# Adaptive-norm transformer layer on one Trainium2 core: the feed-forward part a slot later, local values from whole probabilities and a value difference, gate logits in column strips, and a split rank product

## The reference, cut to what matters

```python
h = layernorm(x) * (1 + ca) + sa
x = x + ga * attention(h)
h = layernorm(x) * (1 + cb) + sb
x = x + gb * feed(h)

# attention(h): q = rope(h @ Wq), k = rope(h @ Wk), v = h @ Wv
#   out_comp: softmax over up to 64 compressed keys (one per 16 tokens), masked, times compressed values
#   out_sel:  softmax over 16 selected tokens (the two blocks of highest mean score), times their values
#   out_win:  softmax over the last 128 tokens (cols <= rows, cols > rows - 128), times v
#   g = softmax(h @ Wg + bg, axis=-1)                      # 3 gates per token
#   out = g[0] * out_comp + g[1] * out_sel + g[2] * out_win
#   return out @ Wo + bo
# feed(h): base = h @ base_W.T + base_b                    # 512 x 512
#   z = h @ [shared_A, routed_A].T                         # 16 + 6 * 16 = 112 columns
#   routed z weighted by the normalised top 2 of 6 router probabilities
#   return base + [z_shared, z_routed * w] @ [shared_B, routed_B].T
```

## Time and profile before

| | |
|---|---|
| median of 3 runs | 2219.99 us (2219.48 to 2226.52) |
| the profiled execution's own time | 2229.21 us |
| its span, first to last instruction | 2227.3 us |
| mean granted TensorE clock | 0.967 of full speed |
| busy share of the span | PE 91%, PEld 66%, DVE 81%, ACT 60%, POOL 39% |

### The profile page before, as it was taken

How to read it: one execution, slowest core, us unless ns; L and a number is a source line. 1 busy time by engine, 2 the same in 40 slices (tenths; PEclk the granted TensorE clock), 3 DMA queues, 4 the chain that set the end, 5 groups by cost and what they waited for, 6 DMA issues and landing times.

```text
span 2227.3 us, 49222 instructions
## 1 busy us (share of the span) xinstructions
PE 2023.9 (91%) x18028; PEld 1465.2 (66%) x18028; DVE 1793.5 (81%) x4806; ACT 1327.9 (60%) x4658; POOL 878.8 (39%) x843
## 2 busy tenths in 40 slices
PE   6988999899999999989999999999999999987876
PEld 3656667666676766667666666766766676665554
DVE  4668888878987888878897788878898788886775
ACT  2346666556665666655666566655666566655654
POOL 1534444334442444334443344434444344432232
PEclk9999999999999999989999999999999999997888
DMA  6210100101011010110001001010001100010000
GB/s 215 63 44 20 30 25 29 44 25 30 20 34 44 20 30 25 33 40 25 25 25 53 15 30 30 30 39 25 29 20 34 44 25 25 29 32 23 20 20 20
DMA packets 43537, 77.56 MB, mean 35 GB/s; under 512 B 7314, under 2 KB 7314, under 8 KB 43299
## 3 DMA queue, kind: packets, MB, share of 16 engines
q1 hardware_dynamic: 32034, 56.85, 8.9%
q10 hardware_dynamic: 11264, 17.57, 2.1%
HBM read 53.38 MB, written 16.83 MB: 32 GB/s over the span
## 4 chain that ended last, share of the span: by engine, by line
PE 51%; DVE 34%; ACT 6%; issue 5%; POOL 2%; DMA 1%; SPq 1%; DVEq 0%; ACTq 0%; POOLq 0%
DVE ps_s L1791 6%; PE ps_o L685 5%; PE ps_t L660 5%; DVE wmax L1796 4%; PE ps_o L715 4%; PE ps_m L558 3%; PE ps_m L560 3%; PE ps_m L559 3%; PE ps_s L679 3%; PE ps_m L755 3%; PE ps_m L773 3%; PE ps_m L774 3%; PE ps_m L782 3%; PE ps_s L636 3%; PE ps_m L790 2%
## 5 line engine op out<-in xcount | busy, mean ns | idle before, releaser
L1182 ACT ACTIVATE pw<-ps_s,wmax 128x128 f32<-128x128 f32 x1024 | 359.3, 380 | 229.6 <-DVE wmax L1796 227.8
L558 PE MATMUL ps_m<-w_hi,h_hi 128*128 128x512 f32 x768 | 340.8, 444 | 8.6 <-DVE h_lo L1927 4.8
L1192 ACT ACTIVATE pw<-pw,wden 128x128 f32<-128x128 f32 x1024 | 313.7, 400 | 30.5 <-DVE wden L1806 30.5
L560 PE MATMUL ps_m<-w_hi,h_lo 128*128 128x512 f32 x768 | 303.2, 395 | 0.0
L559 PE MATMUL ps_m<-w_lo,h_hi 128*128 128x512 f32 x768 | 302.4, 394 | 0.0
L1182 ACT ACTIVATION_READ_ACCUMULATOR pw<-ps_s,wmax 128x1 f32 x1024 | 225.5, 220 | 0.0
L1817 DVE COPY_PREDICATED pT<-keep_prev,ps_t 128x512 f32<-128x512 uint32 x224 | 166.0, 741 | 68.9 <-PE ps_t L660 68.4
L1478 POOL TENSOR_TENSOR css<-css,cden 128x256 f32<-128x256 f32 (+7 forms) x128 | 123.1, 982 | 207.0 <-DVE cden L1856 207.0
L558 PEld LDWEIGHTS ps_m<-w_hi,h_hi 128*128 128x128 f32 x768 | 145.3, 189 | 71.7 <-issue 44.3
L1819 DVE COPY_PREDICATED pT<-keep_own,ps_t 128x512 f32<-128x512 uint32 x256 | 185.3, 724 | 1.0 <-issue 0.3
L685 PE MATMUL ps_o<-pT,v_s 128*32 128x128 f32 x3840 | 168.3, 283 | 13.8 <-DVE pT L1817 8.9
(11 more groups left out here) (213 smaller groups left out, 4791.4 us busy)
## 6 DMA issues: line engine op xcount, KB each, us to landing
xa<-x_in SPq DMA_DIRECT2D x65, 256.0 KB, 2.7
xc<-x_in SPq DMA_DIRECT2D x64, 256.0 KB, 2.7
out<-xc ACTq DMA_DIRECT2D x64, 256.0 KB, 2.0
gbc<-gate_rows SPq DMA_DIRECT2D x24, 256.0 KB, 3.4
pw<-wmod_in SPq DMA_DIRECT2D x3, 1024.0 KB, 8.2
pT<-wmod_in SPq DMA_DIRECT2D x3, 1024.0 KB, 7.2
qT<-wqkv_in SPq DMA_DIRECT2D x2, 1024.0 KB, 13.6
cv_two<-csv SPq DMA_DIRECT2D x16, 128.0 KB, 3.1
```

Source lines behind the costliest of these rows:

```text
L558: pe_.matmul(ps[:], h_hi[:, c, :], w_hi[:, col, c, :], start=(c == 0), stop=False)
L560: mm = pe_.matmul(ps[:], h_lo[:, c, :], w_hi[:, col, c, :], start=False, stop=(c == NC - 1))
L1182: ins = act.activation(pw[:, hw, :], ps_w[:, j, i, 1, :], ACT.Exp, bias=wmax[:, hw:hw + 1], accum_out=wden[:, 0, hw:hw + 1])
L1192: act.activation(pw[:, hw, :], pw[:, hw, :], ACT.Copy, scale=wden[:, 2, hw:hw + 1]).then_inc(wn_ok, 1)
```

## The change

1. **Feed-forward part a slot later.** `transpose_z`, `feed`, `feed_low`, `feed_up`, `final` and `store` of a tile move from the slot of its `output` to the next one and stand at its head: on PE behind `cs_scores` and ahead of `output`. The residual `x1` gets two buffers. `last` has two feed-forward parts. All lists of all engines are put in new orders; `V` is spread over the places where the feed-forward part stood.
2. **Window values.** `ps_t` is copied out whole by ACT (`probs_all`, into `pT_all`); POOL multiplies this copy by the 0/1 mask (`pT_own`) and makes `vd = v_s[t] - v_s[t-1]` once a slot (`value_change`). PE adds `v_s[t-1]` with `pT_all` and `vd` with `pT_own`: the same number of products. The two masked copies on DVE go. For tile 0 only `pT_all` with `v_s[0]` is used, and the product with zeros that opened the bank goes.
3. **Gate logits.** Wg padded to 32 columns is the stationary operand, `hT` streams (128 columns), and the four parts of the contraction go to four column strips; ACT copies the strips (`gate_strips`), and one product with a 0/1 matrix of 3 columns adds them (`gate_sum`, unit G2).
4. **Rank product split.** z and B become high and low parts: three float32r products in place of one float32 product. ACT writes `zT_hi`, DVE `zT_lo` (`lower_z`).
5. Smaller: `cv_two` and `cv_four` share one buffer `cv_rep`, filled twice a sequence; setup copies move.

```diff
-SLOT_ORDER = [("Y", 1), ("Q", 0), ("K", 1), ("QT", 0), ("G", 0), ("H2T", 0), ("Z", 0), ("KT", 1),
-              ("F", 0), ("ZT", 1), ("V", 1), ("HT", 0)]
+SLOT_ORDER = [("F", 0), ("ZT", 1), ("Y", 1), ("Q", 0), ("K", 1), ("G", 0), ("QT", 0), ("G2", 0),
+              ("H2T", 0), ("V", 1), ("Z", 0), ("KT", 0), ("HT", 0)]
...
-            def gate_logits(seg, b, t, chunks=range(NC)):
...
-                    mm = pe_.matmul(ps[:, 0:3], hT[:, c, :], wg_s[:, c, :], start=(c == 0), stop=(c == NC - 1))
+            def gate_logits(seg, b, t):
...
+                    mm = pe_.matmul(ps[32 * c:32 * c + 32, 0:P], wg_w[:, c, :], hT[:, c, :], start=True, stop=True,
+                                    skip_group_check=True)
+                mm.then_inc(full, 1)
+
+            def gate_sum(seg, b, t):
+                pe_.wait_ge(*m_free_at(seg, b, "G2", t))
+                ps, full = m_target(seg, b, "G2", t)
+                pe_.wait_ge(*m_done_at(seg, b, "G", t))
+                pe_.matmul(ps[:, 0:3], gs[:, :], strip_sum[:, :], start=True, stop=True).then_inc(full, 1)
...
             def window_values(b, t, g):
...
+                pe_.wait_ge(ta_done, n + 2)
+                mm = add_values(g, v_s[:, max(t - 1, 0), :], pT_all[:, g % 2], t > 0 or g == 0, False)
                 if t:
-                    pe_.wait_ge(tw_done, 2 * n + 2)
-                    add_values(g, v_s[:, t - 1, :], pT_prev[:, g % 2], True, False)
-                pe_.wait_ge(tw_done, 2 * n + 3)
-                add_values(g, v_s[:, t, :], pT_own[:, g % 2], False, False).then_inc(pvw_done, 1)
+                    if g == 0:
+                        pe_.wait_ge(vd_ok, (NT - 1) * b + t + 1)
+                    pe_.wait_ge(to_done, split_before(b, t, g) + 2)
+                    mm = add_values(g, vd[:], pT_own[:, g % 2], False, False)
+                mm.then_inc(pvw_done, 1)
...
             def feed_up(seg, b, t):
...
-                pe_.matmul(ps[:], zT[:, :], wb_s[:, :], start=False, stop=True).then_inc(full, 1)
+                pe_.matmul(ps[:], zT_hi[:, :], wb_hi[:, :], start=False, stop=False)
+                pe_.matmul(ps[:], zT_hi[:, :], wb_lo[:, :], start=False, stop=False)
+                pe_.matmul(ps[:], zT_lo[:, :], wb_hi[:, :], start=False, stop=True).then_inc(full, 1)
...
             # TensorE, slot
                 cs_scores(b, s)
-                output(seg, b, t, [0])
+                feed(seg, b, t, [0, 1, 2, 3])
+                feed_low(seg, b, t, [0, 1])
+                transpose_z(seg, b, t)
                 window_scores(b, s, 0)
-                output(seg, b, t, [1, 2, 3])
+                feed_low(seg, b, t, [2, 3])
+                feed_up(seg, b, t)
+                output(seg, b, t, [0, 1, 2, 3])
                 output_low(seg, b, t, [0, 1, 2, 3])
                 project(seg, b, t, "Q", 0, [0, 1, 2, 3])
                 window_scores(b, s, 1)
...
             # ScalarE
+            def probs_all(b, t, g):
+
+                n = 4 * (NT * b + t) + g
+                act.wait_ge(tw_full, n + 2)
+                if n > 1:
+                    act.wait_ge(pvw_done, n)
+                act.activation(pT_all[:, g % 2], ps_t[:], ACT.Copy).then_inc(ta_done, 1)
+
+            def gate_strips(seg, b, t):
+                act.wait_ge(*m_full_at(seg, b, "G", t))
+                ps, done = m_bank(seg, b, "G", t)
+                act.activation(gs[:, :], ps[:, 0:P], ACT.Copy).then_inc(done, 1)
...
             # ScalarE, slot, whole, new
+                copy_zT(seg, b, t)
+                window_exp(b, s, 0)
+                cs_exps(b, s)
+                window_norm(b, s, 0)
+                gate_strips(seg, b, t)
+                probs_all(b, s, 0)
+                copy_qT(seg, b, t)
+                window_exp(b, s, 1)
+                store(b, t)
+                gate_exp(Ta)
+                h_scaled(seg, b, t, "H2T", h2T, mod_c, modc_ok, b + 1)
+                probs_all(b, s, 1)
+                probs_copy(b, s, 0)
+                window_norm(b, s, 1)
+                copy_z(seg, b, t)
+                probs_copy(b, s, 1)
+                probs_all(b, s, 2)
+                copy_kT(seg, b, t)
+                router_exp(b, t)
+                probs_copy(b, s, 2)
+                probs_all(b, s, 3)
+                h_scaled(seg, b, t + 1, "HT", hT, mod_a, moda_ok, ba + 1)
+                probs_copy(b, s, 3)
+                split_h2(seg, b, t)
+                copy_out(b, s)
+                split_h(seg, b, t + 1, Ta + 1, t)
+                copy_v(seg, b, t)
...
             # GpSimd
+            def split_probs(b, t, g):
+
+                n = 4 * (NT * b + t) + g
+                gp.wait_ge(ta_done, n + 2)
+                gp.wait_ge(pvw_done, n)
+                gp.tensor_tensor(pT_own[:, g % 2], pT_all[:, g % 2], keep_own[:].unsqueeze(1).broadcast_to([P, 4, P]),
+                                 ALU.mult).then_inc(to_done, 1)
+
+            def value_change(b, t):
+
+                gp.wait_ge(pvw_done, 4 * (NT * b + t) + 1)
+                gp.tensor_tensor(vd[:], v_s[:, t, :], v_s[:, t - 1, :], ALU.subtract).then_inc(vd_ok, 1)
...
             # GpSimd, slot
+                value_change(b, s)
                 lower_a(b, t)
                 residual_in(b, t)
                 cs_subtract(b, s)
+                rotate(seg, b, t, Ta, "Q", ra)
                 deviation_c(NT * b + t)
-                rotate(seg, b, t, Ta, "Q", ra)
+                split_probs(b, s, 0)
                 cs_normalise(b, s)
+                split_probs(b, s, 1)
                 rotate(seg, b, t, Ta, "K", kr)
+                deviation_a(Ta + 1)
+                split_probs(b, s, 2)
+                split_probs(b, s, 3)
+                weigh_keys(seg, b, t, Ta)
                 lower_h2(b, t)
-                weigh_keys(seg, b, t, Ta)
-                deviation_a(Ta + 1)
                 split_h(Ta + 1)
...
             # VectorE
-            def split_probs(b, t, g):
...
-                if t:
-                    dve.copy_predicated(pT_prev[:, g % 2], keep_prev[:].unsqueeze(1).broadcast_to([P, 4, P]), ps_t[:]
-                                        ).then_inc(tw_done, 1)
-                dve.copy_predicated(pT_own[:, g % 2], keep_own[:].unsqueeze(1).broadcast_to([P, 4, P]), ps_t[:]
-                                    ).then_inc(tw_done, 1 if t else 2)
...
+            def lower_z(seg, b, t):
...
+                dve.tensor_tensor(zT_lo[:, :], ps[0:NZ + 1, 0:P], zT_hi[:, :], ALU.subtract).then_inc(done, 1)
...
             # VectorE, slot
                 cs_mask(b, s)
                 cs_max(b, s)
+                lower_z(seg, b, t)
                 window_max(b, s, 0)
+                final(seg, b, t)
                 residual(seg, b, t)
                 window_weights(b, s, 0)
...
```

More of the change, by code:

```diff
@@ L972, in end_first @@
                 t = 0
+                transpose_z(seg, b, t)
                 window_scores(b, 1, 0)
+                window_scores(b, 1, 1)
                 transpose_cs(b, 0, 0)
+                feed(seg, b, t, [0])
                 cs_values(b, 0, 0)
@@ L1585, in head @@
                 split_h(t + 1)
-                weigh_keys(seg, b, t, t)
-                lower_part(t)
                 if t + 2 < NT:
                     deviation_a(t + 2)
+                weigh_keys(seg, b, t, t)
             def end_first(seg, b):
                 t = 0
+                residual_in(b, t)
                 cs_normalise(b, 0)
+                value_change(b, 1)
                 lower_a(b, 0)
-                residual_in(b, t)
+                cs_subtract(b, 1)
+                split_probs(b, 1, 0)
+                cs_normalise(b, 1)
+                split_probs(b, 1, 1)
                 deviation_c(NT * b + t)
-                cs_subtract(b, 1)
+                split_probs(b, 1, 2)
+                split_probs(b, 1, 3)
                 lower_h2(b, t)
-                cs_normalise(b, 1)
             def end_slot(seg, b, s):
```

737 lines of the change are left out of this document (392 added, 345 removed).

## The result

The changed kernel takes 2077.06 us at the median (2073.64 to 2078.28, 4 runs), the kernel before 2222.97 (2219.48 to 2226.52, 4 runs): a ratio of 0.934, 95% interval 0.932 to 0.937. The prediction was 2100 us. The profiled execution has a span of 2075.8 us against 2227.3, 151.5 us less.

What follows compares the result with a forecast made beforehand. Prediction: in a middle slot DVE is as full as PE. Gains of 67 (middle slots), 35 (first slots), 7 (turns), 6 (epilogue) and 4 (prologue), 119 us, give 2110 on the profiled execution, 2100 at the median; range 2045 to 2195.

Steps and rivals of the forecast that it cites:

- DVE is as full as PE: Middle slot before the change: DVE runs nearly without a gap, 28.55 of 31.14 us, and each engine waits for the other.
- The middle slots: Slots 2 to 7 of seven sequences: from 31.14 to 29.5 us each, 42 x 1.6 = 67 us off.
- the layout: Middle slot's second half: Q rotated until 14.7 us, exponentials from 16.1, ACT's list until 27.1, POOL's mask, values, end 29.5.
- PE's own work would end at 27.9: Middle slot: PE's work, put at 28.3 us, falls by 0.4, so ACT's order in the second half comes late next.
- DVE's sum: Middle slot: masked copies take 5.0 us off, lower_z adds 0.3; DVE goes from 28.55 to 23.9 and bounds no more.
- R4: Rival: POOL holds DVE back for all 6.4 us it gains, middle slots lengthen, kernel takes 2245 us; chance 0.04.
- the sign that the prediction had named for it: Sign of R4: DVE operations of 0.2 us that last 0.9 by the dozen.
- held for half of it, nothing of my sum changes: Within R4: if POOL holds DVE for only half of the 6.4 us, the forecast gains stay as summed.
- The first slot: First slot of each sequence, 41.0 us: less 1.33, most of 2.86, two of 4.9 for the clock; 5 us, 35 in all.
- The turn: Turn between sequences: its own chain bounds it, DVE's four copies go; 1 us off, from -2 to +3, 7 in all.
- The epilogue: Epilogue: longest wait, 3.29 us ahead of half 1, stays; feed fills later ones; 6 us off, from 0 to 20.
- The prologue: Prologue: 8 x 0.25 us for gates and two for setup, 4 us off.

Runs made afterwards that it cites:

- b_dve: Kernel before, with the output projection's product with the gate row done twice on VectorE in each of 42 middle slots: 2260.52 us, ratio 1.018.
- s_act: Changed kernel, with the second copy of compressed and selected probabilities made twice on ScalarE in each of 42 middle slots: 2098.95 us, ratio 0.943.
- s_dve: Changed kernel, with the output projection's product with the gate row done twice on VectorE in each of 42 middle slots: 2104.32 us, ratio 0.945.
- i2: i1, plus VectorE's first-half weights ahead of the residual's statistics and, in closing slots, feed's high products ahead of half 1's scores: 2145.49 us, ratio 0.967.
- i1: Changed kernel, with weighing and summing of keys moved into the next slot, some feed-forward products behind half 0's scores, closing slots' maxima reordered: 2120.13 us, ratio 0.954.
- u_masks: Changed kernel with the window values undone: two masked copies per group on VectorE again, no ScalarE whole copies or GpSimd masking: 2260.1 us, ratio 1.016.
- s_pe: Changed kernel, with the first product of Q, K and V issued twice on TensorE in each of 42 middle slots: 2094.05 us, ratio 0.941.
- s_pool: Changed kernel, with the masking of the second group's probabilities done twice on GpSimd in each of 42 middle slots: 2111.85 us, ratio 0.948.
- u_gates2: Changed kernel with gate logits again by eight small products of 3 columns, placed where the sum of the strips stood: 2093.35 us, ratio 0.942.
- u_rank: Changed kernel with one full-precision rank product on TensorE again in place of three split ones: 2082.9 us, ratio 0.938.
- i3: Changed kernel, with keys' weighing and sum moved into waits of the next slot, and i1's TensorE order at the slot's head: 2076.12 us, ratio 0.934.

## Why the prediction was right, and where its terms were off

The time was forecast as 2100 us and is 2077; the gain on the profiled execution, 151.5 us, is 32.5 above the 119 of the sum. First slots and turns together have 19 of the difference, the epilogue 12, the middle slots 7, and the prologue takes 5 back.

*What bounded the kernel before.* "DVE is as full as PE" holds: b_dve paid 0.62 of 0.69 us in a slot at full clock.

*The middle slots* were predicted at 29.5 us and are 29.3 in slot 3 (29.9 on the average of slots 2 to 6, where they took 31.5 before at full clock); 73.8 us in all (61.7 + 12.1), against 67. The way there was the forecast one up to ACT's list: Q rotation, POOL, transposes, `qT`, half 1's exponentials. Each station lay within 0.4 us of the layout, ACT had no gap from the exponentials to the last `probs_all` but 0.16, and s_act, s_dve and i2 against i1 show that the ring through ACT holds the slot and not TensorE alone. The last link was another one. POOL's last mask, which the layout had as the end, is ready 0.6 us before TensorE comes to it, and the waits of PE over the loop have none for it; ACT's list acts on the slot by the bank `ps_t`, as s_act shows. u_masks shows that the gain needs the second part. "PE's own work would end at 27.9" is the weak sentence: 29.30 less the 0.7 us of waiting found above gives some 28.6 (an estimate), and s_pe paid 0.67 of 0.70 us in slot 3. That 29.5 came out is in part luck: TensorE's work, put too low by 0.7 us, and ACT's tail end nearly together.

*DVE's sum* was the term that was wrong. The prediction took 5.0 us off a slot, put 0.3 in, and gave every other operation its old duration: 28.55 to 23.9, some 1460 us in all. The busy time in slot 3 fell from 27.07 to 24.83, and is 1642.5 in all. Small operations got longer where they now meet one of POOL. The same instruction before and after, by line, with the shortest, median and longest duration in ns:

```profile
L1908 DVE TENSOR_TENSOR zr<-zs,ro x64: 257/258/260, 191.2 to 2220.9; 128x96 f32<-128x96 f32 x64
```

```profile
L2124 DVE TENSOR_TENSOR zr<-zs,ro x64: 257/1281/1396, 193.1 to 2068.6; 128x96 f32<-128x96 f32 x64
...
L2054 DVE TENSOR_SCALAR cm<-cm x64: 181/552/1322, 160.1 to 2031.4; 128x32 f32<-128x32 f32 x64
```

`zr` was never held before and is held in most slots now, up to the end of a POOL operation of 1.28 us; `cm`, at 182 at the median before, is at 552. By the groups of lines `zr` grew by 49 us over the execution, the two operations on `ro` by 53 and `cm` by 20, together 122 of the 182 that are missing. This is the mechanism of R4, with the sign that the prediction had named for it, and the prediction's "held for half of it, nothing of my sum changes" came out: 2 to 3 us a slot of holding, and the forecast time. Nor is more work on GpSimd free: s_pool paid 0.56 of its operation in slots 2 to 6. What the slot would take with no holding at all was not measured; in slot 3 TensorE's products up to the Q rotation leave it 0.04 us there. The rule of the Trainium skill (SBUF — State Buffer, "Who interferes with whom") agrees with these rows, also in what isn't held: the reductions of 128x512 (0.68) and the operations with one operand in PSUM (0.68) keep their duration beside a busy GpSimd. The same section names `tensor_scalar` among the operations that can take both port pairs with one input, and `cm` is one.

*The first slot* was taken at 5 us and gave 10.4 a sequence by the table; by TensorE's list, as the prediction cut it, the slot of the fourth sequence went from 41.03 to 30.4. The window from `cs_scores` is 31.75 us with PE busy for 31.74, at clock 1.00. The prediction named three sums, 1.33, 2.86 and 4.9 for the clock, 9.1 together, and took 5. Both waits are gone from the trace, and with them the whole of the clock's part and not two fifths of it. I read this from the traces; no run separates the three.

*The turn* was taken as a gain of 1. By TensorE's list it gained 0.8; the loss of 1.8 by the cut at `cs_scores` (29.10 to 30.82) is work that stood behind this cut before and stands ahead of it now. First slot and turn together gave 8.7 us a sequence against 6 predicted.

*The epilogue* gained 18 against 6. The view of PE's waits over it, in all, times and longest, first of the kernel before, then of the changed one:

```profile
PE ps_s L647 <- ACT pw L1182: 19.6, 6, 3.4
PE ps_m L755 <- ACT h2T L1134: 13.5, 8, 1.7
PE ps_m L747 <- DVE xc L1728: 5.8, 2, 3.9
PE ps_o L715 <- DMA cv_four<-csv: 4.1, 1, 4.1
```

```profile
PE ps_s L674 <- ACT pw L1270: 24.0, 7, 5.3
PE ps_m L782 <- ACT h2T L1222: 6.4, 8, 1.7
```

The wait ahead of half 1 stayed, as predicted, and grew. The others mostly went, the one for the four small copies of the compressed values with them, which the prediction had taken into account for the first slots alone. No run undoes a part in the epilogue alone, so which edit gave this stays open. *The prologue* gained nothing of its 4 us; I looked for no cause.

*The small parts.* Gates: 0.43 + 0.28 against 0.42 + 0.23 predicted; the old form in a bank that is freed soon costs 16.3 us by u_gates2. Rank product: 5.8 us by u_rank, against 64 x 0.15 = 10.

## What to carry to other kernels

Read a slot as a ring of queues and not by its busiest engine: of an operation more, the middle slots paid all of it on DVE at 79% busy, 0.91 on ACT at 70% and 0.74 on PE at 94%. When a move of work gains nothing, look for what else arrives at the same station: in i3 VectorE was ready for more, and TensorE's last product of Q came no earlier. When work goes from VectorE to GpSimd, list VectorE's operations on SBUF operands (two of them, or one in a `tensor_scalar`) in the stretches where GpSimd will be busy, and give each the length of what it may wait for. Where a bank is shared, the place of its reader can cost more than the products: the old gate logits cost 250 us in the one bank and 16 in the other. Ask of every bank who frees it, where that stands in its engine's queue, and what is queued behind the next taker.
